# One step of a recurrence in eight pipelined stages: its matrix row and sum move to PSUM, six normalizations move from VectorE to ScalarE

## The chip, the cores and the metric

The kernel runs on one core of one Trainium2 chip. Its five engines run side by side: TensorE (PE) multiplies matrices into PSUM, VectorE (DVE) and ScalarE (ACT) work elementwise, GpSimd (POOL) does small elementwise work on SBUF, and SyncE (SP) issues DMAs. Each engine has one queue that it works through in order; engines wait for one another by semaphores. The metric is the time of one execution in microseconds, from the device's clock.

## The reference, cut to what matters

The input x has 8 sequences of 1024 tokens of width 256. Four blocks follow one another, each added to its input, each behind a normalization over the 256 columns (subtract the mean, divide by the standard deviation):

```
x = x + attn_a(norm(x))      # gated linear attention with its own norm, then a GELU layer
x = x + ffn(norm(x))         # mixture of 8 experts, top 2   (m1 in the kernel)
x = x + attn_b(norm(x))      # recurrence:  h = tanh(x_t B + h A^T);  y = h C W_out^T + b_out
x = x + ffn(norm(x))         # the same mixture again        (m2 in the kernel)
```

The recurrence of `attn_b` has a state of 16 numbers for each of the 8 sequences, and 1024 steps that can only be done one after another.

## The kernel before, in words

The 1024 tokens are cut into 32 rounds of 32 tokens for all 8 sequences, so a round is 256 rows of x (two tiles of 128 partitions). A round passes through eight stages, and while one round is in stage 7, the next is in stage 6, and so on: every iteration of the program works on eight rounds at once. Eight iterations are written out at the start, 24 are a loop, seven are written out at the end. Each engine's order of instructions in an iteration is written by hand in its `body`; `live(it, k)` says that stage k has work in this iteration. Between those instructions stand the 32 steps of the recurrence, one after another. ScalarE's and TensorE's bodies are cut at another point of the round than VectorE's, so the same round has another number there.

**A step** k of the recurrence is three pieces on two engines:

- VectorE, `spread_state(k)` (L853): waits for the tanh of step k-1 and turns the state into rows, `h_row`, by a 32x32 transpose (L856).
- VectorE, `sum_state(k)` (L858): multiplies `h_row` by the matrix rows `a_by_out` and sums over 32 columns into `sum_h` (L861, in the profile as CUSTOM_DVE_ANT_0 and, for the sum, DVE_READ_ACCUMULATOR2_ANT).
- ScalarE, `state_of(k)` (L556): `hs[:, k] = tanh(sum_h + u[:, k])` (L562), with `u` the projected inputs of the round. `u` is copied from PSUM by `keep_inputs` (L564) once TensorE's `project_inputs` has made them.

All of these lie in SBUF, except the inputs before `u`. Whatever stands between two steps in an engine's order delays the next step if it takes longer than the step's way through the other engine.

**The normalizations.** VectorE makes mean and variance (`stats`, `moments`), GpSimd makes 1/std (`rstd`, L392, with a pow; L396) and, where ScalarE does the normalization, also the shift -mean/std (two more operations, L399 and L403). On VectorE the normalization is `normed` (L883, L884), a subtraction and a multiplication by pointers, for `y0` (from `xin`, after GpSimd's chain `inner_rstd` of seven operations, L405 to L420), `xhat` (from `xag`, the same rows loaded again) and `y1` (from `xmid`). Two halves each, so six a round. On ScalarE it is `normed` (L570, L572), for `ym1`, `ym2` (inputs of the two mixtures) and `yr` (input of the recurrence). `y0`, `ym1`, `ym2`, `y1` and `yr` are transposed by TensorE afterwards (L1328). `keep_norm` (L428) keeps mean and 1/std for `xhat`.

**The output of the recurrence.** GpSimd adds the bias, `x2b = m1.acc + bout` (L503). TensorE's `read_out` (L1348) multiplies the states of the round by `cw` into two PSUM banks, and VectorE adds `x2b` (L1051) into `m2.x`, the input of the second mixture.

**PSUM banks** are shared by hand (`BANK`, `BANK_ORDER`): before a product goes into a bank, TensorE waits for the last reader of the bank's previous use. `combine` (L887, L893) is VectorE's weighted sum of expert outputs from PSUM.

## Time and profile before

| | |
|---|---|
| median of 2 runs | 1887.74 us (1886.91 to 1888.57) |
| the profiled execution's own time | 1882.85 us |
| its span, first to last instruction | 1881.1 us |
| PE busy | 1558.0 us (83% of the span) |
| DVE busy | 1507.9 us (80%) |
| ACT busy | 1096.5 us (58%) |
| POOL busy | 860.8 us (46%) |
| mean granted TensorE clock | 0.935 of full speed |

Busy times of different engines overlap. The numbers of the stages with the recurrence repeat every round, so one round of the loop, read instruction by instruction, stands for 24. Times in the timeline rows are microseconds from the span's start; a duration in a timeline row can overlap the next row's start by some 0.1 us, since instructions of an engine are started before the last has drained. "L861" is line 861 of the kernel.

### The profile page before, as it was taken

To read this page: it belongs to the slowest core of one execution; us is meant where nothing else is said; L and a number is where in the kernel's file an instruction comes from. 1 tells how busy PE (TensorE), PEld (TensorE's weight loads), DVE (VectorE), ACT (ScalarE), POOL (GpSimd) and SP (SyncE) were. 2 spreads that over 40 slices of the span, in tenths; PEclk is the share of its full clock that TensorE was granted. 3 is DMA by queue.
4 is the path that set the end of the run, shared out by engine and by line. 5 is a ranking of instruction groups with operands and counts; after the bars stand their busy time and mean duration, and the time that the engine had idled before them with its cause. 6 is when DMAs were issued, how large, how long until landed. Compare 5 with 4: busy or idle time off the path is not lost.

```text
span 1881.1 us, 52703 instructions
## 1 busy us (share of the span) xinstructions
PE 1558.0 (83%) x17160; PEld 1210.6 (64%) x17160; DVE 1507.9 (80%) x6602; ACT 1096.5 (58%) x2823; POOL 860.8 (46%) x1325
## 2 busy tenths in 40 slices
PE   4687989888888888888878888888898888898866
PEld 3566767666666666666666666666666666776644
DVE  3577888888888888888888888888888888887775
ACT  4556665656665555665555666555666555665542
POOL 2554454445445445445445444445545445544321
PEclk8798999999999999999999999999999999898988
DMA  5211111111011111011111011111111111100000
GB/s 153 70 58 38 42 42 52 51 51 40 24 43 47 51 51 43 31 34 45 51 51 47 27 38 42 51 51 48 32 34 40 51 51 51 40 30 24 7 12 12
DMA packets 118152, 82.50 MB, mean 44 GB/s; under 512 B 42801, under 2 KB 109009, under 8 KB 117841
## 3 DMA queue, kind: packets, MB, share of 16 engines
q1 hardware_dynamic: 116992, 80.15, 13.9%
q14 instruction: 146, 1.19, 0.2%
q8 instruction: 38, 0.62, 0.1%
q10 hardware_dynamic: 976, 0.54, 0.1%
HBM read 47.11 MB, written 33.55 MB: 43 GB/s over the span
## 4 chain that ended last, share of the span: by engine, by line
DVE 34%; issue 30%; ACT 12%; POOL 11%; PE 9%; DMA 2%; DVEq 1%; SPq 1%; POOLq 1%; ACTq 1%
DVE a_h L861 8%; PE ps L1322 7%; DVE h_row L856 4%; DVE stage L893 4%; DVE acc L893 3%; ACT hs L562 3%; POOL stage L503 2%; POOL acc L426 1%; POOL part L424 1%; POOL r L396 1%; ACT stage L572 1%; DVE xmid L1124 1%; POOL ra L396 1%; DVE stage L1051 1%; POOL ra L418 1%
## 5 line engine op out<-in xcount | busy, mean ns | idle before, releaser
L1322 PE MATMUL ps<-we,yT 128*128 128x512 f32 x3072 | 827.2, 417 | 44.0 <-DVE stage L893 27.4
L1322 PEld LDWEIGHTS ps<-we,yT 128*128 128x128 f32 x3072 | 578.6, 198 | 216.6 <-DVE stage L893 39.4
L562 ACT ACTIVATE hs<-sum_h,u 128x1 f32<-128x1 f32 x1024 | 299.6, 293 | 543.4 <-DVE sum_h L861 525.3
L861 DVE CUSTOM_DVE_ANT_0 a_h<-a_by_out,h_row 128x32 f32<-128x32 f32 x1024 | 308.1, 301 | 24.2 <-issue 13.7
L856 DVE STREAM_TRANSPOSE h_row<-hs 128x32 f32<-128x32 f32 x1024 | 207.4, 203 | 139.5 <-ACT hs L562 71.7
L893 DVE SCALAR_TENSOR_TENSOR acc<-ps,coef,acc 128x256 f32<-128x256 f32 x384 | 181.8, 473 | 42.3 <-POOL acc L426 40.9
L893 DVE SCALAR_TENSOR_TENSOR stage<-ps,coef,stage 128x256 f32<-128x256 f32 x384 | 179.6, 468 | 10.6 <-POOL stage L426 5.6
L517 POOL TENSOR_TENSOR orstd<-omean,mhalf 128x32 f32<-128x32 f32 x32 | 174.3, 5447 | 0.2
L424 POOL TENSOR_TENSOR stage<-stage 128x256 f32<-128x256 f32 x64 | 47.1, 736 | 222.3 <-ACT stage L585 222.3
L424 POOL TENSOR_TENSOR part<-part 128x256 f32<-128x256 f32 x64 | 47.1, 736 | 202.1 <-ACT part L585 199.7
L1322 PE MATMUL ps<-wa,hTs 128*128 128x512 f32 x384 | 101.8, 403 | 36.0 <-ACT stage L585 35.9
L1322 PEld LDWEIGHTS ps<-h2Ts,wa 128*128 128x128 f32 x768 | 99.1, 192 | 28.3 <-DVE acc L893 21.4
L1322 PE MATMUL ps<-h2Ts,wa 128*128 128x256 f32 x768 | 105.4, 287 | 13.7 <-DVE acc L893 10.3
L1322 PEld LDWEIGHTS ps<-wa,hTs 128*128 128x128 f32 x384 | 70.6, 190 | 61.1 <-ACT stage L585 47.2
L1322 PE MATMUL ps<-wa,gTs 128*128 128x256 f32 x768 | 107.2, 289 | 1.7 <-ACT ktok L638 1.1
L1322 PEld LDWEIGHTS ps<-wa,gTs 128*128 128x128 f32 x768 | 94.6, 188 | 20.8 <-issue 17.9
L511 POOL TENSOR_SCALAR omean<-oss 128x32 f32<-128x32 f32 x32 | 8.9, 278 | 193.3 <-DVE oss L1225 193.3
L1328 PE MATMUL ps<-cst,stage 128*128 128x128 f32 x256 | 49.7, 327 | 42.9 <-ACT stage L572 38.1
L861 DVE DVE_READ_ACCUMULATOR2_ANT sum_h<- 128x1 f32 x1024 | 82.8, 81 | 0.1
L394 POOL TENSOR_SCALAR ra<-mv_a 128x2 f32<-128x2 f32 x32 | 6.2, 192 | 163.0 <-DVE mv_a L880 163.0
L576 ACT ACTIVATE ps<-ps,lnb,lnw 128x256 f32<-128x256 f32 x128 | 66.9, 526 | 20.7 <-PE ps L1328 20.5
L1360 PE MATMUL ps<-yT,rw 128*32 128x256 f32 x512 | 50.1, 470 | 34.4 <-DVE yT L956 34.4
(176 smaller groups left out, 3209.3 us busy)
## 6 DMA issues: line engine op xcount, KB each, us to landing
arow<-att SPq DMA_DIRECT2D x32, 512.0 KB, 2.8
atx<-arow SPq DMA_DIRECT2D x128, 128.0 KB, 2.9
vrow<-vtok SPq DMA_DIRECT2D x32, 256.0 KB, 2.2
vx<-vrow SPq DMA_DIRECT2D x128, 64.0 KB, 2.0
out<-stage SPq DMA_DIRECT2D x64, 128.0 KB
xin<-in_x SPq DMA_DIRECT2D x62, 128.0 KB
xag<-in_x SPq DMA_DIRECT2D x62, 128.0 KB
stage<-in_experts SPq DMA_DIRECT2D x1, 2048.0 KB, 9.4
```

Source lines behind the costliest of these rows:

```text
L396: g.tensor_tensor(buf[:, 1, :], buf[:, 0, :], mhalf[:, 0:TILES], ALU.pow).then_inc(sem(f"rstd_{name}"), 1)
L424: g.tensor_tensor(m.part[:, i, 0, :], m.part[:, i, 0, :], m.part[:, i, 1, :], ALU.add).then_inc(sem(f"part{m.s}"), 1)
L503: g.tensor_tensor(x2b[:], m1.acc[:], bout[:].unsqueeze(1).broadcast_to([P, TILES, D]), ALU.add).then_inc(sem("x2b"), 1)
L517: g.tensor_tensor(orstd[:], omean[:], mhalf[:], ALU.pow).then_inc(sem("orstd"), 1)
L562: a.activation(hs[:, k:k + 1], sum_h[:], ACT.Tanh, bias=u[:, k:k + 1]).then_inc(sem("rnn_tanh"), 1)
L576: a.activation(ps[:, bank, c * TOK:(c + 1) * TOK], ps[:, bank, c * TOK:(c + 1) * TOK], ACT.Identity, bias=lnb[:, c:c + 1], scale=lnw[:, c: ...
L856: v.transpose(h_row[:], hs[:, last:last + 1].broadcast_to([P, PAIR])).then_inc(sem("rnn_row"), 1)
L861: v.tensor_tensor_reduce(a_h[:], a_by_out[:], h_row[:], 1.0, 0.0, ALU.mult, ALU.add, sum_h[:]).then_inc(sem("rnn_sum"), 1)
L893: v.scalar_tensor_tensor(m.acc[:, i, :], ps[:, bank, half * D:(half + 1) * D], m.coef[:, i, e:e + 1], m.acc[:, i, :], ALU.mult, ALU.add).t ...
L1322: ins = t.matmul(dst, left(lp, c), right(rp, c), start=(n == 1), stop=(n == 3 * chunks))
L1328: ins = t.transpose(ps[:, dst_bank, c * TOK + i * P:c * TOK + (i + 1) * P], src[:, i, c * P:(c + 1) * P], ident)
L1360: ins = t.matmul(ps[ROUTED * g:ROUTED * (g + 1), bank, 0:TOK], rw[:, c, :], m.yT[:, part, c, :].bitcast(F32), start=True, stop=True, skip_ ...
```

## The change

`sum_h` and a copy of the matrix rows (`a_kept`) lie in a PSUM bank of their own (bank 5), which the attention output and the read-out give up by each using one full bank instead of halves of two. The input `u[:, k]` is no longer the bias of the tanh but the starting value of VectorE's sum, so `sum_state(0)` waits for `u`. The six normalizations `y0`, `xhat`, `y1` are ScalarE's, and GpSimd makes a shift for each pair. The running sum `m1.acc` is copied by ScalarE to `x2b`, later by ScalarE from there into the read-out's bank, where TensorE's read-out is added; `bout` is added by VectorE with that sum. The mixture's semaphores are renamed and counted together (`WEIGH`), with the same waits. The order of the sequences in the recurrence's partitions changes (`row_of`), and the read-out is 4 products of 512 columns instead of 8 of 256.

```diff
     def sum_state(k, count):                                  # VectorE
         dve.wait_ge(sem("rnn_row"), past((count - 1) * TS + k + 1))
-        v.tensor_tensor_reduce(a_h[:], a_by_out[:], h_row[:], 1.0, 0.0, ALU.mult, ALU.add, sum_h[:]).then_inc(sem("rnn_sum"), 1)
+        if k == 0:
+            dve.wait_ge(sem("u"), count)
+        v.tensor_tensor_reduce(a_h[:], a_kept, h_row[:], 1.0, u[:, k:k + 1], ALU.mult, ALU.add, sum_h).then_inc(sem("rnn_sum"), 1)
     def state_of(k, count):                                   # ScalarE
         if k == 0:
-            act.wait_ge(sem("u"), count)
             act.wait_ge(sem("RO"), past(count - 1))
         act.wait_ge(sem("rnn_sum"), past((count - 1) * TS + k + 1))
-        a.activation(hs[:, k:k + 1], sum_h[:], ACT.Tanh, bias=u[:, k:k + 1]).then_inc(sem("rnn_tanh"), 1)
+        a.activation(hs[:, k:k + 1], sum_h, ACT.Tanh).then_inc(sem("rnn_tanh"), 1)
+a_kept, sum_h = ps[:, BANK["STEP"], 0:PAIR], ps[:, BANK["STEP"], PAIR:PAIR + 1]
...
     # GpSimd, inner_rstd: two more operations behind the last
+    g.tensor_tensor(ra[:, 2, :], ra[:, 6, :], mv_a[:, :, 0], ALU.mult).then_inc(sem("inner_step"), 1)
+    g.tensor_scalar(ra[:, 3, :], ra[:, 2, :], -1.0, 1.0, ALU.mult, ALU.mult).then_inc(sem("shift_a"), 1)
     # keep_norm
-    g.tensor_tensor(nrm[:, 0, :], mv_a[:, :, 0], one[:, 0:TILES], ALU.mult).then_inc(sem("nrm"), 1)
+    g.tensor_tensor(nrm[:, 0, :], mv_a[:, :, 0], ra[:, 1, :], ALU.mult).then_inc(sem("nrm"), 1)
+    g.tensor_scalar(nrm[:, 2, :], nrm[:, 0, :], -1.0, 1.0, ALU.mult, ALU.mult).then_inc(sem("shift_x"), 1)
-    rstd(mv_f, rf, "f", c3)
+    rstd(mv_f, rf, "f", c3, True)
-    g.tensor_tensor(x2b[:], m1.acc[:], bout[:].unsqueeze(1).broadcast_to([P, TILES, D]), ALU.add).then_inc(sem("x2b"), 1)
...
     # ScalarE, body
         state_of(29, c7)
+        act.wait_ge(sem("onorm"), c4)
+        act.wait_ge(sem("x2b"), c7)
+        act.wait_ge(sem("x3"), past(c7 - 1))
+        a.activation(ps[:, RO, :], x2b[:].rearrange("p i d -> p (i d)"), ACT.Copy).then_inc(sem("x2"), 1)
         state_of(30, c7)
...
         state_of(3, c6)
+        act.wait_ge(sem("x2"), past(c6 - 1))
+        act.wait_ge(sem("mv_r"), c6)
+        a.activation(x2b[:], m1.acc[:], ACT.Copy).then_inc(sem("x2b"), 1)
+        act.wait_ge(sem("shift_a"), c2)
+        normed(y0, xin, ra, 0, 6, 3).then_inc(sem("y0"), 1)
         state_of(4, c6)
+        normed(y0, xin, ra, 1, 6, 3).then_inc(sem("y0"), 1)
...
+        act.wait_ge(sem("shift_f"), c4)
+        normed(y1, xmid, rf, 0).then_inc(sem("y1"), 1)
         state_of(11, c6)
+        normed(y1, xmid, rf, 1).then_inc(sem("y1"), 1)
         state_of(12, c6)
...
         gelu(1).then_inc(sem("gT"), 1)
+        act.wait_ge(sem("shift_x"), c3)
+        act.wait_ge(sem("x_again"), c3 * 16 * TILES + X_FIRST)
+        normed(xhat, xag, nrm, 0).then_inc(sem("xhat"), 1)
         state_of(22, c6)
+        normed(xhat, xag, nrm, 1).then_inc(sem("xhat"), 1)
...
     # VectorE, body
-    dve.wait_ge(sem("x2b"), c6)
-    v.tensor_tensor(m2.x[:], recurrent, x2b[:], ALU.add).then_inc(sem("x3"), 1)
+    v.tensor_tensor(m2.x[:], ps[:, RO, :].rearrange("p (i d) -> p i d", i=TILES), bout[:].unsqueeze(1).broadcast_to([P, TILES, D]), ALU.add).then_inc(sem("x3"), 1)
```

Taken out of VectorE's body are the six `normed`; the first `mask_scores` moves in front of step 5, the second in front of step 6. `xmid` now also waits for `xhat`.

Three places of the order, first **ScalarE from the tanh of step 3 to that of step 6** (`hs` is the tanh, `stage<-stage,r` is `ym2`, `ps<-ps` the attention read-out). Before:

```order
L562 ACTIVATE hs<-sum_h,u 128x1
L561 REGISTER_ALU
L562 ACTIVATE hs<-sum_h,u 128x1
L572 ACTIVATE stage<-stage,r 128x256
L561 REGISTER_ALU
L562 ACTIVATE hs<-sum_h,u 128x1
L596 ACTIVATE ps<-ps 128x2x2x64
L668 ISA
L596 ACTIVATE ps<-ps 128x2x2x64
L671 REGISTER_ALU
L572 ACTIVATE ym<-mx_in,r 128x256
L561 REGISTER_ALU
```

Now:

```order
L567 ACTIVATE hs<-ps 128x1
L668 ACTIVATE stage<-acc 128x512
L670 REGISTER_ALU
L577 ACTIVATE y<-xin,ra 128x256
L566 REGISTER_ALU
L567 ACTIVATE hs<-ps 128x1
L577 ACTIVATE y<-xin,ra 128x256
L577 ACTIVATE stage<-stage,r 128x256
L566 REGISTER_ALU
L567 ACTIVATE hs<-ps 128x1
L601 ACTIVATE ps<-ps 128x2x2x64
```

Three instructions more stand between the tanhs of steps 3 and 5, and the first `y` waits for GpSimd's `shift_a`.

**VectorE from step 9 to `top_two`** (`h_row` and the pair behind it are a step; `stage<-ps,coef,stage` is `combine` of m2). Before:

```order
L856 STREAM_TRANSPOSE h_row<-hs 128x32
L1140 REGISTER_ALU
L892 ISA
L893 SCALAR_TENSOR_TENSOR stage<-ps,coef,stage 128x256
L860 REGISTER_ALU
L861 ISA a_h,sum_h<-a_by_out,h_row 128x32
L861 ISA sum_h 128x1
L884 TENSOR_SCALAR y<-xmid,mv_f,rf 128x256
L856 STREAM_TRANSPOSE h_row<-hs 128x32
L892 REGISTER_ALU
L893 SCALAR_TENSOR_TENSOR stage<-ps,coef,stage 128x256
L860 REGISTER_ALU
```

Now:

```order
L888 STREAM_TRANSPOSE h_row<-hs 128x32
L892 REGISTER_ALU
L895 ISA a_h,ps<-ps,h_row,u 128x32
L895 ISA ps 128x1
L1166 REGISTER_ALU
L923 ISA
L924 SCALAR_TENSOR_TENSOR stage<-ps,coef,stage 128x256
L923 REGISTER_ALU
L924 SCALAR_TENSOR_TENSOR stage<-ps,coef,stage 128x256
L888 STREAM_TRANSPOSE h_row<-hs 128x32
```

The `y1` halves are gone from between the steps, with the wait for GpSimd that the first had, and the two `combine` stand together.

**GpSimd behind the chain of `inner_rstd`.** Before:

```order
L420 TENSOR_TENSOR ra<-ra 128x2 [waits inner_step]
L287 REGISTER_ALU
L394 TENSOR_SCALAR r<-mv 128x2 [waits mv_m2,pads_zero]
L396 TENSOR_TENSOR r<-r,mhalf 128x2 [waits var_m2]
L399 TENSOR_TENSOR r<-r,mv 128x2 [waits rstd_m2]
L403 TENSOR_SCALAR r<-r 128x2 [waits mr_m2,pads_zero]
```

Now:

```order
L422 TENSOR_TENSOR ra<-ra 128x2 [waits inner_step]
L423 REGISTER_ALU
L424 TENSOR_TENSOR ra<-ra,mv_a 128x2 [waits inner_step]
L289 REGISTER_ALU
L428 TENSOR_SCALAR ra<-ra 128x2 [waits inner_step,pads_zero]
L289 REGISTER_ALU
L396 TENSOR_SCALAR r<-mv 128x2 [waits mv_m2,pads_zero]
L398 TENSOR_TENSOR r<-r,mhalf 128x2 [waits var_m2]
L401 TENSOR_TENSOR r<-r,mv 128x2 [waits rstd_m2]
L405 TENSOR_SCALAR r<-r 128x2 [waits mr_m2,pads_zero]
```

The shifts of m2 and, behind it, of m1 stand two operations later.

## Rows read from the trace of the kernel before

**Rows 1.** The page: the span, and shares of the chain that ended last.

```profile
span 1881.1 us, 52703 instructions
...
DVE 34%; issue 30%; ACT 12%; POOL 11%; PE 9%; DMA 2%; DVEq 1%; SPq 1%; POOLq 1%; ACTq 1%
```

**Rows 2.** Windows of a round: stretch, length, busy PE, PEld, DVE, ACT, POOL, clock, DMA.

```profile
950.00:1006.00 56.00, 46.18 (x536) 35.97 (x536) 46.94 (x207) 33.62 (x88) 26.77 (x41) 1.00 0.14 43
1062.00:1118.00 56.00, 48.74 (x536) 38.56 (x536) 47.00 (x207) 33.72 (x90) 26.73 (x41) 0.94 0.14 43
```

**Rows 3.** VectorE, timeline: the steps that cut the round (start us, duration us).

```profile
950.01 0.17 DVE L861 CUSTOM_DVE_ANT_0 a_h<-a_by_out,h_row 128x32 f32<-128x32 f32 x1
...
958.42 0.20 DVE L856 STREAM_TRANSPOSE h_row<-hs 128x32 f32<-128x32 f32 x1
...
967.14 0.19 DVE L856 STREAM_TRANSPOSE h_row<-hs 128x32 f32<-128x32 f32 x1
...
976.05 0.19 DVE L856 STREAM_TRANSPOSE h_row<-hs 128x32 f32<-128x32 f32 x1
...
1006.02 0.17 DVE L861 CUSTOM_DVE_ANT_0 a_h<-a_by_out,h_row 128x32 f32<-128x32 f32 x1
```

**Rows 4.** TensorE, timeline: the transpose of m2's logits in that round.

```profile
984.27 0.44 PE L1367 MATMUL ps<-cst,stage 128*128 128x128 f32 x2 [1.88 <-ACT stage L735]
```

**Rows 5.** VectorE by line and shape: busy us, mean ns | idle before, releaser.

```profile
L861 DVE CUSTOM_DVE_ANT_0 a_h<-a_by_out,h_row 128x32 f32<-128x32 f32 x1024 | 308.1, 301 | 24.2 <-issue 13.7
L884 DVE TENSOR_SCALAR y<-xmid,mv_f,rf 128x256 f32<-128x256 f32 x64 | 56.6, 888 | 21.1 <-POOL rf L396 21.1
...
L884 DVE TENSOR_SCALAR y<-xin,mv_a,ra 128x256 f32<-128x256 f32 x64 | 26.1, 409 | 7.5 <-POOL ra L420 7.3 <-issue 0.2
L884 DVE TENSOR_SCALAR xhat<-xag,nrm 128x256 f32<-128x256 f32 x64 | 24.8, 388 | 5.6 <-DMA xag<-in_x 5.6
...
L1245 DVE SCALAR_TENSOR_TENSOR glog<-zb,ge 128x256 f32<-128x256 f32 x32 | 14.1, 441 | 32.5 <-ACT ge L760 32.5
...
L1023 DVE SCALAR_TENSOR_TENSOR sg<-th,ps 128x256 f32<-128x256 f32 x32 | 13.1, 409 | 1.2 <-ACT vtok L591 1.2
...
L849 DVE TENSOR_SCALAR cw<-ps,cst 128x256 f32<-128x256 f32 x2 | 0.8, 460 | 0.0
```

**Rows 6.** Lines L861 and L893: duration ns min/median/max, first and last start.

```profile
L861 DVE CUSTOM_DVE_ANT_0 a_h<-a_by_out,h_row x1024: 156/190/1306, 127.9 to 1849.6; 128x32 f32<-128x32 f32 x171
L893 DVE SCALAR_TENSOR_TENSOR acc<-ps,coef,acc x384: 440/479/487, 110.2 to 1806.5; 128x256 f32<-128x256 f32 x192
```

**Rows 7.** VectorE, timeline: two sums and the first half of `y1`.

```profile
965.31 1.29 DVE L861 CUSTOM_DVE_ANT_0 a_h<-a_by_out,h_row 128x32 f32<-128x32 f32 x1
...
967.56 1.25 DVE L861 CUSTOM_DVE_ANT_0 a_h<-a_by_out,h_row 128x32 f32<-128x32 f32 x1
...
972.77 1.38 DVE L884 TENSOR_SCALAR y<-xmid,mv_f,rf 128x256 f32<-128x256 f32 x1 [0.61 <-POOL rf L396]
```

**Rows 8.** GpSimd, timeline of the same stretch.

```profile
965.14 0.19 POOL L403 TENSOR_SCALAR r<-r 128x2 f32<-128x2 f32 x1 [0.22 <-POOL r L399]
965.29 1.26 POOL L478 TENSOR_TENSOR res<-xag,b 128x512 f32<-128x512 f32 x1
967.36 1.40 POOL L482 TENSOR_TENSOR state<-smid,dstate 128x512 f32<-128x512 f32 x1 [0.80 <-DVE dstate L1105]
...
972.70 1.29 POOL L503 TENSOR_TENSOR stage<-acc,bout 128x512 f32<-128x512 f32 x1
```

**Rows 9.** ScalarE by line and shape, columns as in Rows 5.

```profile
L562 ACT ACTIVATE hs<-sum_h,u 128x1 f32<-128x1 f32 x1024 | 299.6, 293 | 543.4 <-DVE sum_h L861 525.3 <-PE ps L1352 11.7 <-ACT u L568 1.0
...
L572 ACT ACTIVATE stage<-acc,rr 128x256 f32<-128x256 f32 x64 | 37.7, 589 | 0.8 <-POOL rr L403 0.8
...
L617 ACT ACTIVATE eq<-grel 128x256 f32<-128x256 f32 x32 | 12.9, 403 | 4.3 <-DVE grel L964 4.3
```

**Rows 10.** ScalarE, timeline: the copy of the round's inputs.

```profile
956.22 0.20 ACT L568 ACTIVATE u<-ps 128x32 f32<-128x32 f32 x1
```

More of the change, by code:

```diff
@@ L202, in build @@
         hs, u = sb("hs", [P, TS]), sb("u", [P, TS])
-        h_row, a_h, sum_h = sb("h_row", [P, PAIR]), sb("a_h", [P, PAIR]), sb("sum_h", [P, 1])
+        h_row, a_h = sb("h_row", [P, PAIR]), sb("a_h", [P, PAIR])
         ps = ctx.enter_context(nc.psum_tensor("ps", [P, 8, 512], F32))
@@ L235, in build, with row_of @@
         REST = {w: n + 1 for n, w in enumerate(("gate", "early", "scaled_out", "late", "recurrence", "experts0", "experts"))}
-        recurrence_weights = [(a_in[b * N:(b + 1) * N, b % 2 * N:(b % 2 + 1) * N], wts["A"]) for b in range(B)]
+        def row_of(b):
+            return b % BQ * PAIR + b // BQ * N
+        recurrence_weights = [(a_in[row_of(b):row_of(b) + N, b // BQ * N:(b // BQ + 1) * N], wts["A"]) for b in range(B)]
         X_FIRST = 16 * TILES * (BQ - 1)
@@ L568, in keep_inputs, with normed @@
                 a.activation(u[:], inputs, ACT.Copy).then_inc(sem("u"), 1)
[L570 to L572 removed]
+            def normed(dst, src, r, i, scale=1, shift=2):
+                return a.activation(dst[:, i, :], src[:, i, :], ACT.Identity, bias=r[:, shift, i:i + 1], scale=r[:, scale, i:i + 1])
             def affine(bank, name, c):
@@ L881, in moments @@
                 ins.then_inc(sem(f"mv_{name}"), 1)
-            def normed(dst, src, mean, scale, i):
-                return v.tensor_scalar(dst[:, i, :], src[:, i, :], mean[:, i:i + 1], scale[:, i:i + 1], ALU.subtract, ALU.mult)
             def combine(m, k, half, bank, count):
@@ L1122, in body @@
                     dve.wait_ge(sem("WO"), c3)
+                    dve.wait_ge(sem("xhat"), TILES * c3)
                     dve.wait_ge(sem("res_mid"), past(c3 - 1))
@@ L1261, in body @@
                     spread_state(21, c5)
-                if live(it, 2):
-                    normed(xhat, xag, nrm[:, 0, :], nrm[:, 1, :], 1).then_inc(sem("xhat"), 1)
-                if live(it, 5):
                     sum_state(21, c5)
@@ L1340, in project_inputs @@
                     for half in range(2):
-                        for pair in range(B // 2):
-                            b = 2 * pair + half
-                            ins = t.matmul(ps[PAIR * pair:PAIR * (pair + 1), RB, 0:TS], bin_[:, c, (1 - half) * N:(3 - half) * N],
+                        for q in range(BQ):
+                            b = half * BQ + q
+                            ins = t.matmul(ps[PAIR * q:PAIR * (q + 1), RB, 0:TS], bin_[:, c, (1 - half) * N:(3 - half) * N],
                                            yrT[:, c, b * TS:(b + 1) * TS], start=(c == 0 and half == 0), stop=(c == KC - 1 and half == 1),
@@ L1348, in read_out @@
             def read_out():
-                for b in (0, 2, 4, 6, 1, 3, 5, 7):
-                    r = slice(b // 2 * PAIR, (b // 2 + 1) * PAIR)
-                    ins = t.matmul(ps[b % BQ * TS:(b % BQ + 1) * TS, RO + b // BQ, 0:D], hs[r, :], cw[r, b % 2, :], start=True, stop=True)
+                for q in range(BQ):
+                    r = slice(q * PAIR, (q + 1) * PAIR)
+                    ins = t.matmul(ps[q * TS:(q + 1) * TS, RO, :], hs[r, :], cw[r].rearrange("p i d -> p (i d)"), start=False, stop=True,
+                                   skip_group_check=True)
                 return ins
@@ L1404, in attend @@
                     for q in range(BQ):
-                        b, o = i * BQ + q, j * HQ * DV
-                        ins = t.matmul(ps[q * 32:q * 32 + 32, BANK["O"] + i, o:o + HQ * DV], atx[:, b, j * TS:(j + 1) * TS],
-                                       vx[:, b, :, j * DV:(j + 1) * DV], start=(first and j == 0), stop=(j == J - 1),
+                        b, o = i * BQ + q, i * D + j * HQ * DV
+                        ins = t.matmul(ps[q * 32:q * 32 + 32, BANK["O"], o:o + HQ * DV], atx[:, b, j * TS:(j + 1) * TS],
+                                       vx[:, b, :, j * DV:(j + 1) * DV], start=(first and i == 0 and j == 0), stop=(j == J - 1),
                                        skip_group_check=True)
@@ L1495, in body @@
                 if live(it, 6):
-                    stepped, free = value(pe, c6 * TS), [(name, value(pe, count)) for name, count in readers(it, "RO")]
+                    stepped, given = value(pe, c6 * TS), value(pe, c6)
                     pe.wait_ge(sem("pads_zero"), 1)
                     pe.wait_ge(sem("rnn_tanh"), stepped)
-                    for name, count in free:
-                        pe.wait_ge(sem(name), count)
+                    pe.wait_ge(sem("x2"), given)
                     read_out().then_inc(sem("RO"), 1)
@@ L1604, in body @@
                 if live(it, 2):
-                    attend(1, isinstance(it, int) and it == 2).then_inc(sem("O11"), 1)
+                    attend(1, False).then_inc(sem("O11"), 1)
                 if live(it, 4):
```

113 lines of the change are left out of this document (51 added, 62 removed).

## The prediction, made before the changed kernel had run

> **What bounds the kernel now.** The first view is the page. Its chain of waits [rows 1] names VectorE most (34%), then stretches in which an engine waited for nothing that the trace shows (30%), and no other engine with more than 12%. So no unit is full, and the time is a chain that changes engines. The windows come next: a loop round takes 56.0 us, and it takes that with TensorE at full clock and 46.2 us busy as well as at a granted 0.94 and 48.7 us busy [rows 2]. TensorE thus has at least 7 us a round to spare, VectorE 9, ScalarE 22. What sets the round is the recurrence's 32 steps, each through VectorE and ScalarE, with everything that stands between them on VectorE.
>
> The third view is the timeline of VectorE, read for instructions that take longer than their kind. The sum of a step has a median of 190 ns and a maximum of 1306 [rows 6], with a mean of 301 [rows 5]. Its 1.29 and 1.25 us [rows 7] end with GpSimd's 1.26 and 1.40 us additions [rows 8]; the first half of `y1` (1.38 us) starts and ends with GpSimd's `x2b` (1.29). The 384 `combine` of `acc` never exceed 487 ns [rows 6]: one tensor of theirs is in PSUM. **VectorE instructions with all tensors in SBUF stand still while GpSimd works through a long one; those with one tensor in PSUM do not.**
>
> **The change, part by part.** I cut the round at VectorE's rows 950.01, 958.42, 967.14, 976.05 and 1006.02 [rows 3] and at TensorE's 984.27 [rows 4].
>
> The prices: a stalled sum costs (301 - 190) ns x 1024 / 32 = 3.6 us a round [rows 5, 6]; with the matrix row in PSUM it has the form of `combine`, so this goes. A normalization of `y0` or `xhat` costs VectorE 0.41 or 0.39 us, of `y1` 0.89 us [rows 5], plus 0.61 us of wait for GpSimd ahead of the first `y1` [rows 7]: 2 x 0.41 + 2 x 0.39 + 2 x 0.89 + 0.61 = 4.0 us a round. So VectorE is freed of 7.6 us a round.
>
> On ScalarE the six cost 0.59 us each [rows 9]. The two copies of 512 columns to and from `x2b` have no row of their own; between a plain pass over 256 columns, 0.40, and twice that [rows 9], I take 0.6. The tanh loses a pointer: two pointers cost 589 - 403 = 186 ns [rows 9], so one is 90, and 293 becomes 200. ScalarE's load grows by 6 x 0.59 + 2 x 0.6 - 32 x 0.09 = 1.9 us a round, and it had 22 free [rows 2]. What matters is where the new ones stand.
>
> The sum gains the pointer `u`. No row has this instruction with one. `combine`, with a pointer, takes 479 [rows 6] where `sg`, of the same width and without, takes 409 [rows 5]: up to +70 ns; the other end is 0. I take 60. Reading PSUM: `sg` (PSUM) 409 against `glog` (SBUF) 441 says -32 ns, `cw` (PSUM) 460 against `xhat` 388 says +72 [rows 5]. I take 0, since `sg` and `glog` are two-tensor instructions like the sum. Writing `sum_h` to PSUM from VectorE is in no row; these same ends bound it, and I take 0.
>
> The Trainium skill speaks against this ("VectorE: DVE Perf Modes", the TRN2 errata section): a source in PSUM costs VectorE 120 cycles fixed, one in SBUF 58, which is 65 ns more at 0.96 GHz. By that, an estimate from that page, 32 sums would cost 2 us a round more and the forecast would be some 40 us higher; `sg` against `glog` does not show it.
>
> - *950.01 to 958.42.* Step 0's sum now waits for `u`, which ScalarE copies at 956.22 [rows 10], after TensorE's projection, itself behind an expert product. The projection cannot come much sooner, so a stall of 0.6 us regained in this stretch is given back in that wait. The copy into the read-out's bank stands in ScalarE's wait ahead of step 30. Gain 0 (-0.5 to +0.6).
> - *958.42 to 967.14.* VectorE loses half a `y0` (0.4) and one stall (1.29 - 0.19 = 1.1) [rows 7]. But GpSimd's shifts of m2 and m1 stand two operations later. With the waits between them I take 0.64 us (0.19 each without, from L403; 0.19 + 0.22 of wait for the second [rows 8]). The shift of m1, at 965.14 + 0.19 = 965.33 before, comes at 965.97; behind it `ym1` (0.59) and the tanh of step 6 (0.20), then 0.05 to VectorE: 966.9 instead of 967.14. Gain 0.25. On ScalarE the copy and `y0` wait for the same GpSimd chain, so they are inside this.
> - *967.14 to 976.05.* A stall of 1.25 - 0.19 = 1.06 [rows 7, 8], half a `y0` (0.3, overlap taken off), both halves of `y1` and their wait (0.61 + 1.30 + 0.33), another stall (0.5, one of the 3.6 counted): 4.1. ScalarE still has the copies ahead of `hTs` in order, and VectorE will wait for the last of them: I give back 0.8. Gain 3.3.
> - *976.05 to 984.27.* Half an `xhat` (0.3) and a small wait for a tanh (0.2). `y1` on ScalarE hides under the softmax's small VectorE work. Gain 0.5.
> - *984.27 to 1006.02.* Half an `xhat` (0.3), a stalled sum at step 27 (0.95, of which 0.4 counts, as ScalarE's `gTs` copy ends no sooner), two tanhs behind table loads (0.2). Gain 0.9; I take 0.8, because `xhat` on ScalarE stands between two tanhs.
>
> Sum -4.85 us. Against it the pointer: 0.06 x 32 = 1.9 us; in about 20 of the steps VectorE sets the pace, so 1.2. The round becomes 56.0 - 3.65 = 52.35 us. The loop has 24 rounds: -88 us. The recurrence runs in 8 more, less filled; at half each, -15. Before 127.9 us, where the first sum starts [rows 6], six normalizations change place without a recurrence beside them: 0. GpSimd's missing `x2b` (1.29) ends up as its idle time, except for the stall already counted. The 4 products of the read-out instead of 8 move as many columns: 0.
>
> So the profiled execution's 1882.85 us becomes 1780. The median of the timed runs, 1887.74, is 4.9 higher, and that offset should stay: **1785 us**.
>
> **The rivals.**
>
> *A. The waits change place.* ScalarE's queue takes the freed time: `shift_a`, `shift_m2`, `shift_m1` and `shift_f` all stand ahead of a tanh, and TensorE, which would be 48.7 / 52.35 = 93% busy at the lower clock [rows 2], makes the products late. For it: GpSimd is named in the chain with 11% [rows 1]. Against it: ScalarE waits 525 us in total for the sums [rows 9], 0.5 us a step, nearly the length of one normalization. If half of the 3.65 us is lost: 1.8 x 24 + 7 = 51 us, 1837.
>
> *B. The sum goes on standing still*, because the pointer `u` in SBUF counts like a tensor. The change then does not do that part. `combine` has its pointer `coef` in SBUF and a maximum of 487 [rows 6], which speaks against it. Of the stalls, 1.1, 1.06, 0.5 and 0.4 were in my stretches; the first was mostly hidden by GpSimd's chain anyway. Without 2.0 us: 1.65 x 24 + 7 = 47 us, 1841.
>
> *C. PSUM is dear for the small sum.* Each of 32 sums gets longer by p on VectorE, with the pointer's 0.06 on top, and all of them lie on the chain. It decides from p = 3.65 / 32 = 0.11 us: from there the kernel is slower. With `cw`'s +72 for the read and the same again for the write, p = 0.144: 4.6 us against 3.65, +0.95 x 24 + 8 = +31, **1919**. The rule of the Trainium skill named above ("VectorE: DVE Perf Modes", errata) is a p of 65 ns and alone does not reach that point.
>
> *D. More than forecast.* The pointer is free, the waits I gave back are not there: 5.6 us a round, 24 x 5.6 + 20 = 154, 1734.
>
> **How the numbers follow.** Forecast (1745 to 1825) 0.60; A 0.15, B 0.07, C 0.08, D 0.10. The range takes in A and B whole and the upper half of D: 1735 to 1852, with C, half of D and a tail of A outside, under 0.2. A few runs tell 2% from no change: 1850 is the bound of faster, 1925.5 that of slower. Faster: forecast, D and nearly all of A and B, 0.81. Within 2%: the tails of A and B and the nearer half of C, 0.13. Slower: the rest of C, 0.06.
>
> **What the changed profile would show.** The sum's maximum falls from 1306 ns to under 350, its median rises from 190 to some 250, and the tanh's falls from 293 to 200. The first VectorE wait for `u` of 0.5 us or so stands ahead of step 0. A round in the windows takes 52.4 us. VectorE's busy time falls by 107 us of normalizations and 114 of stalls, and rises by 61 for the pointer: 1348. ScalarE's rises by some 60. TensorE's wait for the `ym` and for m2's logits (1.88 us [rows 4]) shrinks. I am wrong if the tanh shows waits for GpSimd's work queued ahead of it of over 1 us, if the sum's median passes 300, or if long sums remain beside GpSimd's additions.

## The result, and the profile after

The changed kernel takes 1802.1 us (1801.4 to 1802.9) against 1887.7: a ratio of 0.955, with a 95% interval of 0.951 to 0.959. The forecast was 1785, its range 1735 to 1852. The sign, the range and the kind of gain were right; 86 of 103 us came. About 4 of the 86 are luck: the profiled executions differ by 81.5 us only (1882.85 and 1801.37), because the offset of 4.9 us between the profiled and the timed runs, which I had kept, is 0.8 here. Behind the agreement stand three things that I had not seen: terms of the loop round that were mis-sized, rounds in which TensorE's clock falls and which the changed kernel feels and the kernel before hardly does, and a pause at VectorE's loop turn that is worth 50 us in both kernels.

The page of after, against [rows 1]: the span, busy time by engine, the instruction queues, and the chain that ended last.

```profile
span 1799.6 us, 52728 instructions
...
PE 1518.5 (84%) x16904; PEld 1178.5 (65%) x16904; DVE 1395.4 (78%) x6411; ACT 1094.9 (61%) x3079; POOL 849.3 (47%) x1453
...
q14 instruction: 147, 1.20, 0.2%
q8 instruction: 38, 0.62, 0.1%
...
issue 30%; DVE 28%; POOL 17%; ACT 15%; PE 5%; DVEq 2%; DMA 1%; POOLq 1%; SPq 1%; ACTq 1%
```

VectorE's share of the chain fell from 34 to 28%, GpSimd's rose from 11 to 17%, and "issue" stayed at 30%: a third of the chain is time in which an engine waited for nothing shown. One round in the windows (columns as in [rows 2]) is 3 us shorter, with VectorE 4.1 us less busy. The round before it, with TensorE's granted clock at 0.94, took 1.7 us longer:

```profile
852.33:907.06 54.73, 49.05 (x530) 37.67 (x529) 42.91 (x200) 33.72 (x96) 26.28 (x45) 0.94 0.14 44
907.06:960.10 53.04, 46.24 (x530) 35.97 (x529) 42.83 (x200) 33.68 (x96) 26.30 (x45) 1.00 0.15 45
```

All of this difference lies between the rows of steps 7 and 11, where TensorE makes products for a mixture. First the two windows, then the wait with which VectorE reads the mixture's transposed logits in the first of them; in the second there is no such wait.

```profile
874.12:881.78 7.66, 6.97 (x30) 4.81 (x31) 5.61 (x25) 3.99 (x12) 4.19 (x8) 0.59 0.50 153
928.84:934.80 5.96, 4.87 (x32) 3.60 (x33) 5.52 (x25) 3.95 (x12) 4.20 (x8) 1.00 0.59 178
```

```profile
881.30 0.23 DVE L932 TENSOR_REDUCE lm<-ps 128x16 f32<-128x64 f32 x1 [1.17 <-PE ps L1377]
```

In the slower window TensorE ran most of the time at 1.2 GHz, the lower of its two levels (0.59 on the mean), in the other at 2.4 GHz, and six products with `we` ahead of that transpose took 2.92 and 1.67 us:

```profile
877.91 2.92 PE L1331 MATMUL ps<-we,yT 128*128 128x512 f32 x6
...
932.19 1.67 PE L1331 MATMUL ps<-we,yT 128*128 128x512 f32 x6
```

In the 12.1 us ahead of either window TensorE was busy 10.48 us at full clock, so no row tells why the clock fell in one and not in the other.

The sum of a step and the read of its accumulator, against [rows 6] (min/median/max in ns):

```profile
L895 DVE CUSTOM_DVE_ANT_0 a_h<-ps,h_row,u x1024: 217/250/254, 124.3 to 1768.5; 128x32 f32<-128x32 f32 x171
L895 DVE DVE_READ_ACCUMULATOR2_ANT ps<- x1024: 132/142/144, 124.5 to 1768.6; 128x1 f32 x171
```

No sum is over 254 ns, where 1306 occurred: the standing still beside GpSimd is gone. The median rose by 60 ns, which run 8 below shows to be the pointer. The second row is new to the argument: writing the sum to PSUM takes 142 ns, and before, to SBUF, it took 82:

```profile
L861 DVE DVE_READ_ACCUMULATOR2_ANT sum_h<- x1024: 73/82/89, 128.0 to 1849.7; 128x1 f32 x171
```

ScalarE, against [rows 9] (busy us, mean ns | idle before, releaser):

```profile
L567 ACT ACTIVATE hs<-ps 128x1 f32<-128x1 f32 x1024 | 172.4, 168 | 467.0 <-DVE ps L895 437.6 <-PE ps L1361 22.7
...
L577 ACT ACTIVATE xhat<-xag,nrm 128x256 f32<-128x256 f32 x64 | 37.8, 596 | 0.0
...
L577 ACT ACTIVATE ym<-mx_in,r 128x256 f32<-128x256 f32 x64 | 36.7, 593 | 14.5 <-POOL r L405 14.5
L577 ACT ACTIVATE y<-xin,ra 128x256 f32<-128x256 f32 x64 | 36.6, 595 | 5.9 <-POOL ra L428 5.4
L577 ACT ACTIVATE y<-xmid,rf 128x256 f32<-128x256 f32 x64 | 36.2, 589 | 3.0 <-POOL rf L405 3.0
```

The tanh takes 168 ns instead of 293, the moved normalizations 589 to 596, and they hardly wait. TensorE's wait for m2's logits, against [rows 4], shrank from 1.88 to 1.49 us:

```profile
943.26 0.44 PE L1377 MATMUL ps<-cst,stage 128*128 128x128 f32 x2 [1.49 <-ACT stage L759]
```

VectorE's waits, over the whole span (us in total, times, longest):

```profile
DVE h_row L888 <- issue: 77.5, 23, 3.6
DVE acc L924 <- POOL acc L434: 47.2, 32, 2.7
DVE h_row L888 <- ACT hs L567: 43.7, 145, 1.0
DVE glog L1257 <- ACT ge L784: 30.0, 31, 3.6
DVE att L981 <- ACT ps L601: 25.5, 30, 0.9
```

The first row is the largest wait of the engine that the chain names most, and its releaser is "issue". It occurs 23 times, and a loop of 24 rounds turns 23 times. The timeline of VectorE at such a turn, first before, then after:

```profile
1000.14 0.21 DVE L856 STREAM_TRANSPOSE h_row<-hs 128x32 f32<-128x32 f32 x1 [2.79 <-issue]
1000.27 0.27 DVE L964 TENSOR_SCALAR grel<-grel 128x256 f32<-128x256 f32 x1
```

```profile
956.70 0.14 DVE L895 DVE_READ_ACCUMULATOR2_ANT ps<- 128x1 f32 x1
960.10 0.21 DVE L888 STREAM_TRANSPOSE h_row<-hs 128x32 f32<-128x32 f32 x1 [3.26 <-issue]
```

VectorE's loop branch lies at 956.67 in after. Step 24's tanh ended at 957.61, so the row of step 25 came 2.5 us later than it could.

### The profile page after: what moved, and what is told of

Its sections match the earlier page's. It is cut to its first block, busy times and chain, and to the rows that moved or that the text cites. A ratio compares the mean times of both kernels' runs of the same rounds, so it can differ in the third digit from the quotient of the medians.

```text
span 1799.6 us, 52728 instructions
## 1 busy us (share of the span) xinstructions
PE 1518.5 (84%) x16904; PEld 1178.5 (65%) x16904; DVE 1395.4 (78%) x6411; ACT 1094.9 (61%) x3079; POOL 849.3 (47%) x1453
## 4 chain that ended last, share of the span: by engine, by line
issue 30%; DVE 28%; POOL 17%; ACT 15%; PE 5%; DVEq 2%; DMA 1%; POOLq 1%; SPq 1%; ACTq 1%
DVE a_h L895 5%; DVE h_row L888 4%; PE ps L1331 3%; DVE acc L924 3%; DVE ps L895 3%; DVE stage L924 3%; POOL r L398 2%; ACT hs L567 2%; ACT qx L612 2%; POOL res L501 2%; ACT L782 2%; POOL res L490 1%; POOL acc L434 1%; POOL part L432 1%; POOL ra L398 1%
## 5 line engine op out<-in xcount | busy, mean ns | idle before, releaser
L1331 PE MATMUL ps<-we,yT 128*128 128x512 f32 x3072 | 801.8, 407 | 42.0 <-DVE stage L924 33.8
L1331 PEld LDWEIGHTS ps<-we,yT 128*128 128x128 f32 x3072 | 560.3, 192 | 202.2 <-DVE stage L924 45.9
L567 ACT ACTIVATE hs<-ps 128x1 f32<-128x1 f32 x1024 | 172.4, 168 | 467.0 <-DVE ps L895 437.6
L895 DVE CUSTOM_DVE_ANT_0 a_h<-ps,h_row,u 128x32 f32<-128x32 f32 x1024 | 251.8, 246 | 42.0 <-ACT u L573 16.0
L895 DVE DVE_READ_ACCUMULATOR2_ANT ps<- 128x1 f32 x1024 | 145.3, 142 | 0.0
L981 DVE TENSOR_TENSOR att<-ps,cst 128x512 f32<-128x512 f32 x64 | 44.1, 691 | 40.8 <-ACT ps L601 25.5
L581 ACT ACTIVATE ps<-ps,lnb,lnw 128x256 f32<-128x256 f32 x128 | 68.0, 535 | 12.1 <-PE ps L1337 11.1
L1370 PE MATMUL ps<-yT,rw 128*32 128x256 f32 x512 | 43.8, 416 | 30.2 <-DVE yT L987 30.2
```

The source lines that it names most:

```text
L567: a.activation(hs[:, k:k + 1], sum_h, ACT.Tanh).then_inc(sem("rnn_tanh"), 1)
L581: a.activation(ps[:, bank, c * TOK:(c + 1) * TOK], ps[:, bank, c * TOK:(c + 1) * TOK], ACT.Identity, bias=lnb[:, c:c + 1], scale=lnw[:, c: ...
L895: v.tensor_tensor_reduce(a_h[:], a_kept, h_row[:], 1.0, u[:, k:k + 1], ALU.mult, ALU.add, sum_h).then_inc(sem("rnn_sum"), 1)
L981: return v.tensor_tensor(att[:].rearrange("p i h (j t) -> p j (i h) t", j=J)[:, j:j + 2], ps[:, SD + j:SD + j + 2, 0:TOK].rearrange("p j ( ...
L1331: ins = t.matmul(dst, left(lp, c), right(rp, c), start=(n == 1), stop=(n == 3 * chunks))
L1370: ins = t.matmul(ps[ROUTED * g:ROUTED * (g + 1), bank, 0:TOK], rw[:, c, :], m.yT[:, part, c, :].bitcast(F32), start=True, stop=True, skip_ ...
```

## The experiments

Each was timed beside the kernel before on the same chip; the ratios are to that kernel. **With the pause** at the turn, or **without**, is stated for each, as the later runs made plain that it must be. "Round" is the mean distance of the 24 loop branches on VectorE: 56.06 us before, 53.51 after.

**1. The normalizations alone.** The step is as before: row and sum in SBUF, `u` as the tanh's bias, ScalarE waits for `u`. The copies to and from `x2b` and the read-out of four products stay as in the changed kernel, here and in run 2.

```diff
-v.tensor_tensor_reduce(a_h[:], a_kept, h_row[:], 1.0, u[:, k:k + 1], ..., sum_h)   # row, sum in PSUM
+v.tensor_tensor_reduce(a_h[:], a_by_out[:], h_row[:], 1.0, 0.0, ..., sum_h)        # row, sum in SBUF
-a.activation(hs[:, k:k + 1], sum_h, ACT.Tanh)
+a.activation(hs[:, k:k + 1], sum_h, ACT.Tanh, bias=u[:, k:k + 1])
```

> The changed kernel with the recurrence's step as it was: matrix row, sum and u in SBUF, u as the tanh's bias. So the normalizations and copies on ScalarE alone. Theory 1 (both parts are needed, and the stalls beside GpSimd's long additions are worth about half): the sum's maximum is again about 1300 ns and its median 190, and the time lies half way, 1835 to 1855. Theory 2 (the step in PSUM is worth nothing, since what its sums win they lose by being longer): 1800 to 1815, no more than 1% above the changed kernel.

1849.0 us, ratio 0.980 (0.978 to 0.981), round 54.62. It lies in the expected interval, by accident: this kernel has no pause (its `h_row` waits 105.9 us for `ACT hs`, and "issue" is absent from its list). Run 11 gives the fair comparison.

**2. The step alone.** The six normalizations are back on VectorE at their places of before (a long edit, not shown); row and sum in PSUM and `u` as start value stay.

> The changed kernel with the six normalizations back on VectorE at their old places (with GpSimd's shifts; x2b stays on ScalarE). Theory 1: 1825 to 1850, since no sum stands still but VectorE has 3.5 us a round more, of which part is hidden. The first half of y1 takes 0.4 us, not 1.38, since GpSimd's x2b addition is gone. Theory 2 (only the normalizations matter): at 1870 or above.

1842.8 us, 0.976 (0.975 to 0.978), round 54.62, with the pause. The sums have a mean of 245 ns, and a half of `y1` takes 442 ns on the mean where it took 888 [rows 5]. As expected.

**3. The matrix row alone back in SBUF.**

```diff
-v.tensor_tensor_reduce(a_h[:], a_kept, h_row[:], ...
+v.tensor_tensor_reduce(a_h[:], a_by_out[:], h_row[:], ...
```

> The changed kernel with the matrix row alone read from SBUF; sum still in PSUM, u still the start value. Theory 1 (the row in PSUM keeps the sum out of GpSimd's way): long sums of up to 1.3 us come back beside GpSimd's 512-column additions, the median stays 250 ns, and the time rises by 1.2 to 2 us a round, to 1830 to 1850. Rival (a pointer in SBUF made the stall, or the row in PSUM costs reading time): the maximum stays under 300 or the median falls to 190, and the time stays or falls.

1919.3 us, 1.017 (1.015 to 1.019), round 57.27, with the pause. One operand's place is worth 117 us, more than the whole change. Its sums:

```profile
L895 DVE CUSTOM_DVE_ANT_0 a_h<-a_by_out,h_row,u x1024: 220/251/1315, 125.2 to 1886.0; 128x32 f32<-128x32 f32 x171
```

The long ones return with the row, though sum and output stay where they were. The mean of 335 against 246 ns is 91 us of the 117. The loop round is 3.76 us longer; by the same rows in both kernels at the same clock it is 2.8 (the rows of steps 28 to 1, 1 to 7 and 7 to 11 come 0.45, 0.85 and 1.51 us later), and the rest goes by way of TensorE's clock, which is low somewhere in rows 7 to 11 in 22 of 23 rounds here and in 5 in the changed kernel. The direction was expected; the size is about three times what I had put down. It also lies above the kernel before, so with the row in SBUF the rest of the change costs time.

**4. `u` back as the tanh's bias**, row and sum in PSUM.

```diff
-if k == 0: dve.wait_ge(sem("u"), count)
-v.tensor_tensor_reduce(a_h[:], a_kept, h_row[:], 1.0, u[:, k:k + 1], ...
+v.tensor_tensor_reduce(a_h[:], a_kept, h_row[:], 1.0, 0.0, ...
-a.activation(hs[:, k:k + 1], sum_h, ACT.Tanh)
+a.activation(hs[:, k:k + 1], sum_h, ACT.Tanh, bias=u[:, k:k + 1])
```

ScalarE waits for `u` ahead of step 0 again.

> The changed kernel with u as the tanh's bias again, the sum starting from 0 and step 0 not waiting for u on VectorE. Theory 1: the sum's main part falls from 250 to 190 ns, the tanh rises from 168 to some 255; VectorE sets the pace in two thirds of the steps, so about 1 us a round is won there and 0.3 to 0.6 lost where the tanh is waited for, and the wait of 0.54 us for u goes: 1780 to 1798. Rival (the chain through both engines counts in every step): +0.03 us a step and nothing from the wait, 1802 to 1825.

1726.6 us, 0.915 (0.913 to 0.916), round 50.18, without the pause: 75 us under the changed kernel and 53 under the lower bound expected. At the turn stands another row, and the instruction queue has another count:

```profile
915.72 0.21 DVE L889 STREAM_TRANSPOSE h_row<-hs 128x32 f32<-128x32 f32 x1 [1.19 <-ACT hs L568]
```

```profile
q8 instruction: 38, 0.62, 0.1%
...
q14 instruction: 32, 0.26, 0.0%
```

The wait is now for the tanh itself, 1.19 us. The packets of q14 are 32 instead of 147: 115 fewer, 5 for each of 23 turns, 0.94 MB in all. The traces show when they move. In the changed kernel, between 300 and 1450 us:

```profile
q14 instruction: 109, 0.89, 0.3%
```

The same view of run 4 has no row of q14. By the trace each packet has 8192 bytes; behind the branch at 956.67 the first two start 0.5 and 1.0 us later, inside the pause, the others 3.9, 12.1 and 36.4 us later. So theory L: the pause is VectorE's code for the next round being fetched again, and it depends on the length or the position of that code. Theory P: it comes with `u` as start value. The next four runs were made for this and for the prices.

**5. The changed kernel, VectorE's loop one instruction shorter** (a repeated pair of waits ahead of `kt` left out).

> The changed kernel, but in VectorE's loop two waits before the product with ek that only repeat waits made earlier in the same round are left out (its arithmetic is unchanged): the loop is one instruction shorter, 312 instead of 313. Theory L, the 3.3 us at each turn of VectorE's loop come from how its code is fetched, which depends on the loop's length or position: the pause between the sum of step 24 and the row of step 25 falls from 3.3 to about 1.2 us, 23 turns x 2 us less = 1755 us (1745 to 1770). Theory P, the pause belongs to taking u as the sum's start value: it stays at 3.3 us and the time at 1802 us (1797 to 1807).

1803.3 us, 0.955 (0.954 to 0.957); "issue" 82.5 us, 147 packets. Nothing moved. This spoke for P, or against length alone.

**6. Run 4 with one wait more in the loop**, at step 12.

```diff
-if k == 0: dve.wait_ge(sem("u"), count)
+if k == 12: dve.wait_ge(sem("u"), count)
```

> The kernel with u as tanh's bias again (1726.6 us), with one wait more in VectorE's loop, at step 12, where what it waits for was ready long before: VectorE has as many instructions as in the changed kernel (313 in the loop). Theory L: the pause of 3.3 us at the turn is back, 1726.6 + 23 x 2 = 1773 us (1755 to 1785). Theory P: no pause without u as a start value, 1727 us (1723 to 1732).

1782.7 us, 0.944 (0.942 to 0.946), round 52.68. A wait that never waits costs 56 us. Its row, and its packets:

```profile
DVE h_row L889 <- issue: 79.6, 23, 3.7
```

```profile
q14 instruction: 147, 1.20, 0.2%
```

P fell with this: here `u` is not the start value. The sums and the tanh are those of run 4 (means 185 and 259 ns there, 186 and 260 here), so 56 us is the price of the pause alone.

**7. Run 4 with the sum in SBUF.**

```diff
-a_kept, sum_h = ps[:, BANK["STEP"], 0:PAIR], ps[:, BANK["STEP"], PAIR:PAIR + 1]
+a_kept, sum_h = ps[:, BANK["STEP"], 0:PAIR], sb("sum_h", [P, 1])[:]
```

> The matrix row in PSUM, u as tanh's bias, and the sum in SBUF. Writing the sum costs 81 instead of 141 ns, tanh reads it in 294 instead of 261 ns: 27 ns a step less, 1024 x 27 ns = 28 us, of which not all is on the path: 1705 us (1695 to 1722). The sum does not stand still behind GpSimd's additions, since that goes with the place of the matrix row alone (median about 185, longest under 350 ns). Rival: the sum's place takes part in it, the long sums of over 600 ns return and the time is over 1735 us.

1720.6 us, 0.911 (0.910 to 0.913), round 50.18, without the pause.

```profile
L894 DVE CUSTOM_DVE_ANT_0 a_h<-ps,h_row x1024: 156/189/194, 124.0 to 1688.8; 128x32 f32<-128x32 f32 x171
L894 DVE DVE_READ_ACCUMULATOR2_ANT sum_h<- x1024: 74/83/88, 124.1 to 1688.9; 128x1 f32 x171
```

The write falls from 141 to 83 ns, the tanh rises from 259 to 291, and the sum's place has no part in the standing still. 6 us come of it, a fifth of the 28 that the arithmetic of a step gives: the loop round did not move.

**8. Run 4 with a start value from a pointer to a column of zeros.** No wait for `u`, the tanh keeps its bias.

> The kernel with u as tanh's bias (1726.6 us), but the sum starts from a pointer to a column of SBUF that holds 0 at all times, so there is no wait for u: the price of a pointer by itself. Theory A: the sum goes from 185 to 246 ns in each of 1024 steps, most of it on the path: +40 to +60 us, 1765 to 1787 us. Theory B, what costs is the wait for u and the turn of the loop, and 60 ns of VectorE hide: under 1745 us.

1822.0 us, 0.966 (0.963 to 0.969), round 53.68. This is 95 us above run 4, beyond both theories, because the added clearing of the column (one VectorE instruction ahead of the loop, the loop unchanged) brought the pause: 147 packets, "issue" 88.9 us. Against run 6, which has the pause too, the pointer alone costs 39 us, 1.0 us a round (run 8's own executions lie between 1816.9 and 1829.8 us). It also speaks for position, since the loop is as long as in run 4 and has one instruction more before it; but its sum differs, and so runs 9 and 10, which leave the loop as it is, are what settles it.

**9. The changed kernel with VectorE's loop moved.** The position was chosen from the eight runs: if code is fetched in pieces of 128 instructions, with an edge where run 4's loop ends, then every loop in three pieces had no pause, and every loop in four had one (in the table below: edges at instruction 686, 814, 942 and 1070, run 4's loop from 758 to 1070).

```diff
 dve.wait_ge(sem("pads_zero"), 1)
+for _ in range(150): dve.wait_ge(sem("pads_zero"), 1)
```

> The changed kernel, with 150 waits for a semaphore that has long been set, put once before VectorE's first work; the built program has 75 instructions more for them, all ahead of the loop, and the loop has its 313 as before. Theory L (fetching of VectorE's loop code depends on where it lies): instruction packets of the queue named q14 fall from 147 to about 32, the pause of 3.3 us at 23 turns goes to about 1.2 us, and the time from 1802 to 1750 us (1745 to 1765). Theory P (the pause comes with the start value u): 1802 to 1806 us, packets 147 or a few more.

1754.1 us, 0.930 (0.928 to 0.932), round 51.17, without the pause: 48 us for nothing but the place of the code. q14 has 33 packets, and no `h_row` waits for "issue".

**10. The kernel before with its loop moved**, in the same way by 60 waits.

> The kernel before, with 60 such waits (30 instructions in the built program) before VectorE's first work. Theory L: the packets of q14 fall from 146 to about 32, the pause of 2.8 us goes to about 1.3 us: 1888 - 23 x 1.5 = 1853 us (1835 to 1862). If the pause were bound to what VectorE computes: 1888 to 1891 us.

1837.3 us, 0.974 (0.972 to 0.976), round 53.96, without the pause: 50 us, in the range expected but 16 us under its number. So the change is worth 86 us with the pause in both kernels and 83 without it in either. Its queue:

```profile
q8 instruction: 38, 0.62, 0.1%
...
q14 instruction: 31, 0.25, 0.0%
```

**11. Run 1 with the pause**, by the wait of run 6.

> The six normalizations moved to ScalarE with the step as before (as in the run of that part alone, 1849.0 us), with the one more wait at step 12 that brought the pause back in the kernel with u as bias. Theory L: the pause is back, 1849 + 45 to 56 = 1894 to 1905 us, so that the normalizations alone give nothing, and the whole gain hangs on the matrix row in PSUM. Theory P, or the normalizations are worth 40 us by themselves: 1849 to 1852 us.

1888.9 us, 1.000 (0.999 to 1.002), round 56.20; the pause is back as theory L says, 5 us under its range. With the pause the normalizations alone gain nothing. Without it they cost: run 1 takes 1849.0 us against 1837.3 of run 10, 54.62 against 53.96 a round. VectorE is 92 us less busy than before (1415.8 against 1507.9), and waits more instead. Four rows of its waits:

```profile
DVE att L982 <- PE ps L1407: 29.6, 32, 6.3
DVE lm L933 <- PE ps L1378: 28.9, 21, 2.8
DVE hTs L988 <- ACT hTs L722: 21.9, 31, 2.1
DVE att L982 <- ACT ps L602: 21.7, 29, 0.8
```

In the kernel before the first two were

```profile
DVE lm L901 <- PE ps L1367: 7.0, 14, 2.4
...
DVE att L950 <- PE ps L1396: 6.2, 5, 2.5
```

and the other two were under 5 us.

**12. Run 7 with a shorter GpSimd chain.** The mean is negated before the root is taken, so one operation is left behind it.

```diff
+g.tensor_tensor(buf[:, 2, :], mv[:, :, 0], minus[:], ALU.mult)      # ahead of the root
-g.tensor_tensor(buf[:, 0, :], buf[:, 1, :], mv[:, :, 0], ALU.mult)
-g.tensor_scalar(buf[:, 2, :], buf[:, 0, :], -1.0, 1.0, ALU.mult, ALU.mult)
+g.tensor_tensor(buf[:, 2, :], buf[:, 1, :], buf[:, 2, :], ALU.mult)
```

> The matrix row in PSUM, u as tanh's bias, the sum in SBUF (1720.6 us), and GpSimd makes each negated mean before the root is taken, so that after it one operation is left where there were two: shifts come about 0.35 us sooner, where ScalarE waited 0.4 to 0.5 us for them twice a round. If the walk over the second half of the round hangs on these: up to 32 x 0.4 us = 13 us less, 1707 us (1704 to 1716). Rival: these waits are covered, since TensorE and the steps set the end there: 1717 to 1724 us.

1720.9 us, 0.912 (0.910 to 0.914), round 50.08. The chain became 0.2 us shorter (1.6 to 1.4 us from its first operation to its last), ScalarE's waits for the shifts of `ym1` and `ym2` fell (from 26.2 to 11.5 us in all), and the time is run 7's: those waits are covered.

Together, with VectorE's instructions ahead of its loop and in it, counted in the built programs:

| kernel | ahead / in loop | q14 packets | us | round |
|---|---|---|---|---|
| before | 801 / 312 | 146 | 1887.7 | 56.06 |
| before, moved (10) | 831 / 312 | 31 | 1837.3 | 53.96 |
| norms alone, pause (11) | 761 / 313 | 147 | 1888.9 | 56.20 |
| norms alone (1) | 758 / 312 | 32 | 1849.0 | 54.62 |
| step alone (2) | 803 / 320 | 147 | 1842.8 | 54.62 |
| after, row in SBUF (3) | 761 / 313 | 147 | 1919.3 | 57.27 |
| after | 761 / 313 | 147 | 1802.1 | 53.51 |
| after, shorter loop (5) | 761 / 312 | 147 | 1803.3 | 53.46 |
| after, moved (9) | 836 / 313 | 33 | 1754.1 | 51.17 |
| `u` as bias, pause (6) | 761 / 313 | 147 | 1782.7 | 52.68 |
| `u` as bias (4) | 758 / 312 | 32 | 1726.6 | 50.18 |
| zero by pointer (8) | 759 / 312 | 147 | 1822.0 | 53.68 |
| `u` as bias, sum in SBUF (7) | 758 / 312 | 33 | 1720.6 | 50.18 |
| the same, shorter shifts (12) | 758 / 312 | 32 | 1720.9 | 50.08 |

## Why the prediction was right, and where it was not

**The size of the loop round is the step that missed.** I had -3.65 us x 24 = -88 and -15 for the rest. The branches say -2.55 x 24 = -61, and -20 for the rest of the span, 81 in all for the profiled executions. By stretch, as means over 19 and 20 loop rounds, cut at the rows of the same steps:

| stretch | before | after | difference | forecast, before the pointer |
|---|---|---|---|---|
| sum 28 to row 1 | 9.26 | 9.59 | +0.33 | 0 |
| row 1 to 7 | 8.57 | 8.41 | -0.16 | -0.25 |
| row 7 to 11 | 9.05 | 6.39 | -2.66 | -3.3 |
| row 11 to the next 28 | 29.17 | 29.15 | -0.02 | -1.3 |

(The first cut is here the row of step 28, a few tenths of a us from its sum. The pointer's +1.2 was forecast for the round, not by stretch; shared out by the steps in each, it makes the forecasts +0.2, 0, -3.15 and -0.7, so the 1.1 us that are missing are 0.5 in rows 7 to 11 and 0.6 behind them.)

The stretch from row 7 to row 11 depends on TensorE's clock, and much more so with the normalizations on ScalarE. Its length in us, in 23 rounds of the loop, first where TensorE had full clock in all of it, then in the others:

| kernel | full clock (rounds) | lower in part (rounds) |
|---|---|---|
| before | 8.91 (4) | 8.89 to 9.23 (19) |
| norms alone, pause (11) | 7.39 to 7.40 (6) | 7.39 to 9.10 (17) |
| step alone (2) | 7.22 to 7.23 (22) | 7.83 (1) |
| after, row in SBUF (3) | 7.47 (1) | 7.46 to 9.18 (22) |
| after | 5.96 (18) | 7.66 (5) |
| `u` as bias, pause (6) | 5.86 (23) | none |

At full clock the stretch fell by 2.95 us, close to the forecast; the five rounds with 7.66 take 0.4 of it back.

- *Stalls beside GpSimd.* Right as a mechanism, and shown: runs 3 and after differ in the row's place alone, and the maximum goes from 1315 to 254 ns. I priced 3.6 us a round; run 3 says 57.27 - 53.51 = 3.76, but 2.8 of it at the same clock, so that the agreement is in part luck. It says 117 us over the whole, so 27 us of it lie outside the loop, where I had given 15 to all parts together. The page "SBUF — State Buffer" of the Trainium skill ("Who interferes with whom") names a port that VectorE and GpSimd share, and says that a VectorE instruction with at most one input in SBUF stays off it; these runs agree, and the pointer in SBUF did not count as a second input (maximum 254 ns).
- *Six normalizations off VectorE, 4.0 us a round.* Here the forecast was wrong in kind. Alone they give 0 with the pause (run 11) and cost 12 us without it (run 1 against run 10). On top of the step in PSUM they give 1842.8 - 1802.1 = 41 us. Over the whole the terms are not a sum: in run 11 VectorE's freed time becomes waits for TensorE's products and ScalarE's copies. In rows 7 to 11 the step alone takes off 1.79 us, the normalizations alone 0.77, both (run 6, `u` as bias) 3.19. But at full clock these are 1.68, 1.52 and 3.05: there the parts do add up, and the clock, lower in 17 of run 11's 23 rounds, takes half of what the normalizations alone gain. In rows 1 to 7 the normalizations alone cost 0.67, and nothing with the row in PSUM. That the long sums hold the rest back there fits these numbers; no run isolates it.
- *The pointer, +60 ns on the sum.* 190 to 250 ns: exact. Its worth, 1.2 us a round forecast, is 1.0 by run 8 against 6. For `u` as start value in all, with its wait and with the cheaper tanh, after against run 6 says +19 us. The loss lies where step 0 waits for `u` (rows 28 to 1, 9.59 against 8.97 us) and in the low clock of rows 7 to 11, not behind them. Since the pointer alone is 39 us there, the cheaper tanh and the later wait give back 20, half of it; ScalarE waits 437.6 us for the sums anyway. So this part of the change is a loss.
- *Reading and writing PSUM, 0 and 0.* The read was right: 189 ns from PSUM in run 7, 190 with the row in SBUF [rows 6]. The rule of the Trainium skill's "VectorE: DVE Perf Modes" (TRN2 errata; an estimate of 65 ns more from its cycles for a source in PSUM) does not show in this instruction, which has one of its two inputs there; the trace decides against it. The write was wrong: +60 ns. Of its effect run 7 shows 6 us, since the tanh from PSUM is 32 ns faster and the loop round does not move. With `u` as start value the sum's place was not tested.
- *Later shifts, 0.64 us behind m1's.* Run 12 took 0.2 us off that chain and changed nothing, so in the final form it lies beside other work. The term may have been too dear; in the changed kernel itself it was not tested.
- *Row 11 to the next 28, -1.3 us forecast and 0 found.* The pause is not the cause: from row 24 to row 28 the kernels with it take 8.30 us (before) and 7.92 (after), the moved ones 6.12 and 5.93, a gain either way. But from row 11 to 24 even the moved kernels differ by +0.29, and it is much the same with `u` as bias (21.16 us in run 9, 21.06 in run 4). The pointer is not the cause either: it adds 0.59 us in this stretch (run 8 against 6), but with `u` as bias and the pause the stretch is 29.39 us long, no shorter than with the start value. What sets that part no run tells, so the cause stays open.
- *What the prediction asked the profile to show*: sum's maximum, median and tanh as forecast (254, 250, 168 against 200); a wait for `u` of 0.54 us ahead of step 0; VectorE busy 1395 instead of 1348 us, where the unforeseen write alone adds 62; ScalarE busy unchanged instead of +60, of which 36 is the tanh, which lost 125 ns and not 90. ScalarE waits for GpSimd's shifts 0.5 us twice a round, under the 1 us at which I would have been wrong. Of the rivals, B and C are out by the sum's rows. A is what happened to the normalizations taken alone, and its TensorE, late at the lower clock, is what the five rounds of 54.8 us show in the changed kernel too. I had read from [rows 2] that a round takes 56.0 us at either clock; that holds before (55.98 us in the rounds at full clock, 56.07 in the others) and did not carry over (53.15 and 54.78). At 1.6 us for 5 rounds it costs 8 us here, and far more in run 3.

**What I overlooked.** A wait without a releaser, once in each of 23 turns and the same from round to round, was worth half of each of my two large terms. It did not spoil the forecast only because both kernels had it, which is luck. The "issue 30%" of the page [rows 1] would not have shown it: that share is still 28% in run 10, 25% in run 9 and 31% in run 1, which have no pause. The list of waits shows it.
